# A graph network on one core: one block for all stages, and the first edge group of a relational pass done inside the node pass before it

## The reference, cut to what matters

```python
h = jnp.maximum(_layernorm(x), 0.0)
# twice (w1, sl1, b1, then w2, sl2, b2):
xt  = jnp.einsum('nd,rde->rne', h, W)            # 8 relations
agg = segment_sum(xt[edge_type, src], dst)
h   = relu(agg + h @ SW + b)
x = x + h
h = jnp.maximum(_layernorm(x), 0.0)
e   = relu(concat([h[src], h[dst], edge_attr]) @ eW1 + eb1)
msg = layer_norm(relu(e @ eW2 + eb2), eg, ebeta)
agg = segment_sum(msg, dst)
upd = relu(concat([h, agg]) @ nW1 + nb1) @ nW2 + nb2
out = x + layer_norm(h + upd, ng, nbeta)
```

## Time and profile before

| | us |
|---|---|
| median of the 3 runs | 2733.24 |
| profiled execution, its own time | 2735.01 |
| its span, first to last instruction | 2733.3 |
| TensorE busy | 2139.7 (78%) |
| VectorE busy | 2024.7 (74%) |
| ScalarE busy | 1544.4 (57%) |
| GpSimd (POOL) busy | 1788.3 (65%) |

### The profile page before, as it was taken

One profiled execution on the slowest core, in us unless ns is written; L12 is line 12 of the kernel. 1 busy time (PEld: TensorE's weight loads), 2 busy tenths in 40 slices (PEclk: granted clock), 3 DMA queues, 4 the chain that ended last, 5 costly groups with the idle time before them and its releaser, 6 DMA issues. The chain is left out here.

```text
span 2733.3 us, 54746 instructions
## 1 busy us (share of the span) xinstructions
PE 2139.7 (78%) x16219; PEld 1874.0 (69%) x16219; DVE 2024.7 (74%) x6853; ACT 1544.4 (57%) x3284; POOL 1788.3 (65%) x1381
## 2 busy tenths in 40 slices
PE   3777999999588898888891656577777777648997
PEld 3667999999577798888891655544455544436775
DVE  6887888888333587666662888688777777747999
ACT  4997666666333354444442888645444444426887
POOL 7771777776577188888876777568888888860000
PEclk9999999999899999999995898889888899879999
DMA  6994455555299634444545999877777777739998
GB/s 210 318 323 161 96 103 107 109 109 107 31 340 358 215 73 76 77 85 79 82 56 141 406 417 417 341 230 218 196 189 206 197 200 196 201 72 352 408 409 339
DMA packets 296009, 563.74 MB, mean 206 GB/s; under 512 B 88628, under 2 KB 145377, under 8 KB 295905
## 3 DMA queue, kind: packets, MB, share of 16 engines
q1 hardware_dynamic: 186144, 484.03, 50.9%
q0 software_dynamic: 109760, 78.51, 18.2%
HBM read 368.35 MB, written 205.52 MB: 210 GB/s over the span
## 5 line engine op out<-in xcount | busy, mean ns | idle before, releaser
L1049 POOL DMA_INDIRECT s<-E_summed,c_scat x392 | 637.4, 1626 | 250.9 <-issue 101.5
L1278 PE MATMUL ps<-c_w,E_masked 128*128 128x128 f32 x6272 | 720.4, 276 | 3.9 <-DVE E_masked L1081 3.8
L1278 PEld LDWEIGHTS ps<-c_w,E_masked 128*128 128x128 f32 x6272 | 711.8, 193 | 4.7 <-DVE E_masked L1081 4.7
L1081 DVE SCALAR_TENSOR_TENSOR E_masked<-E_type_row,E_hT 128x512 f32<-128x512 int32 x784 | 483.2, 687 | 78.0 <-ACT E_hT L1198 64.8
L358 POOL DMA_INDIRECT gathered<-s,c_src x392 | 419.0, 1069 | 166.7 <-issue 116.1
L1410 POOL DMA_INDIRECT s<-E_summed,c_scat x196 | 337.4, 1722 | 85.5 <-issue 58.2
L1400 POOL DMA_INDIRECT E_ends<-h,c_near x196 | 202.6, 1034 | 75.8 <-issue 56.1
L358 POOL DMA_INDIRECT gathered<-in_x,c_src x196 | 189.6, 967 | 88.0 <-issue 58.8
L564 PE MATMUL ps<-c_sl,N_hT 128*128 128x128 f32 x1568 | 195.3, 278 | 19.4 <-DVE N_out L399 17.8
L1293 PE MATMUL ps<-E_msg,E_same 128*128 128x128 bf16 (+1 forms) x2450 | 207.3, 241 | 1.2 <-DVE E_msg L1131 1.2
L564 PEld LDWEIGHTS ps<-c_sl,N_hT 128*128 128x128 f32 x1568 | 183.4, 192 | 28.3 <-ACT N_hT L513 21.3
(11 more groups left out here) (133 smaller groups left out, 4461.7 us busy)
## 6 DMA issues: line engine op xcount, KB each, us to landing
s<-N_out SPq DMA_DIRECT2D x147, 512.0 KB, 4.7
N_xin<-in_x SPq DMA_DIRECT2D x98, 512.0 KB, 10.1
N_sin<-s SPq DMA_DIRECT2D x98, 512.0 KB, 6.9
E_dst_row<-in_dst_line SPq DMA_DIRECT2D x147, 256.0 KB, 4.7
E_type_row<-in_type SPq DMA_DIRECT2D x98, 256.0 KB, 4.0
N_xin<-s SPq DMA_DIRECT2D x49, 512.0 KB, 6.4
h<-N_h SPq DMA_DIRECT2D x49, 512.0 KB, 7.8
E_base<-s SPq DMA_DIRECT2D x49, 512.0 KB
```

Source lines behind the costliest of these rows:

```text
L1049: pool.indirect_dma_start(s, bass.IndirectOffsetOnAxis(ap=c["scat"][:, k:k + 1], axis=0), summed[:, g % 2, t * D:(t + 1) * D], None, bound ...
L1081: nc.vector.scalar_tensor_tensor(out=masked[:, u % 2, r, :], in0=type_row[:, u, :], scalar=float(r), in1=hT[:, u % 2, :], op0=ALU.is_equal ...
L1278: ins = nc.tensor.matmul(ps[:, 2 + u % 2, t * D:(t + 1) * D], masked[:, u % 2, r, t * P:(t + 1) * P], w[:, r, :], start=(r == 0 and t == 0 ...
```

## The change

- All stages but the setup stand in one block. `node_product`, `edge_pass_relational` and the others now return a `Stage` of functions, one for each engine, which are called in order in one `nc.Block()`. What the block ends gave is now waited for by name: SP waits for all scatters of an edge pass (`sums_done`) before the first load of the node pass behind it, and POOL waits for the node pass's stores (`all_stored`) before it goes on to the edge pass.
- Group 0 of E1 is worked inside N0, and group 0 of E2 inside N1, by `early_sync`, `early_vector`, `early_scalar` and `early_tensor`, called at the end of each node step: the row loads at step 32, group 0's and 1's statistics, normalisation or copy, and transposes at steps 32 to 41, the masks of groups 0 and 1 two at a time at steps 41 to 48, and group 0's eight products two at a time at steps 43 to 46. In the edge pass TensorE then begins with half of group 1's product and the pairs of group 0.
- The early transposes and products use PSUM banks 6 and 7. The node pass keeps one pair of output banks, 4 and 5, and its product waits half by half for the copy of the group before.
- The node buffers `xin`, `hT` and `out` of N0 and N1 lie in the last 16 slots of `gathered`. So N0 gathers up to group 32 only (N0_AHEAD), and the remaining gathers of an edge pass are spread over its first 42 groups (GATHER_STEPS).
- The node passes' loop ends at group 32 (NODE_LOOP_END = 8); the rest is written out.

The diff without the lines that only move to another indentation:

```diff
-N0_AHEAD = 40
+N0_AHEAD = 32
+NODE_LOOP_END = 8
+GATHER_STEPS = 42
...
-def sweep(eng, step):
+def sweep(eng, step, begin=0, loop_end=LOOP_END):
...
-def node_product(nc, sb, sem, c, ps, a, name, x, s, w, norm, gathers):
+def node_product(nc, sb, sem, c, ps, a, name, x, s, w, norm, gathers, edges, sums_done):
-    xin = sb(f"{name}_xin", [P, UNROLL, NT * D])
-    hT = sb(f"{name}_hT", [P, 2, NT * D])
-    out = sb(f"{name}_out", [P, 2, NT * D])
+    spare = gathers.rows[:, (GROUPS_E - 16) * GE:].rearrange("p (k d) -> p k d", d=NT * D)
+    out, hT, xin = spare[:, 0:2, :], spare[:, 2:4, :], spare[:, 4:8, :]
...
-            copy(out[:, u % 2, h * 512:(h + 1) * 512], ps[:, 4 + 2 * (u % 2) + h, :]).then_inc(out_ready, 1)
+            copy(out[:, u % 2, h * 512:(h + 1) * 512], ps[:, 4 + h, :]).then_inc(out_ready, 1)
...
+                if sums_done:
+                    sp.wait_ge(sums_done, 64 * GROUPS_E)
...
+            edges.early.sync(sp, UNROLL * i + u)
...
     gathers.issue(pool, x, GT * (N0_AHEAD if norm else N1_AHEAD))
+        all_stored(pool, stored)
...
-                wait(pe, out_ready, 2 * (g - 1))
                 for h in range(2):
+                wait(pe, out_ready, 2 * (g - 1) + h + 1)
...
+    def early_sync(sp, at):
+        if isinstance(at, int) and at == 32:
+            for k in range(3):
+                load(sp, 0, k)
...
+        landed = gathers.issued
         for g in range(GROUPS_E):
-                gathers.issue(pool, x, gathers.issued + (1 if norm else 2))
+            gathers.issue(pool, x, TILES_E - (TILES_E - landed) * max(0, GATHER_STEPS - 1 - g) // GATHER_STEPS)
             scatter(g)
...
+    def early_vector(dve, at):
+        if not isinstance(at, int):
+            return
+        if norm and at in (32, 33):
+            k = at - 32
+            rows_here(dve, 0, k)
...
+        if norm and at in (36, 37):
+            shifts(dve, 0, at - 36)
+        if 41 <= at <= 48:
+            masks(dve, 0, (at - 41) // 4, range((at - 41) % 4 * 2, (at - 41) % 4 * 2 + 2))
...
+    def early_scalar(act, at):
+        if not isinstance(at, int):
+            return
+        if norm and at in (33, 34):
+            ln.deviations(nc, act, c["eps"], at - 33, at - 33)
+        if at in (37, 38):
+            if norm:
+                normalise(act, 0, at - 37)
+            else:
+                fetched(act, 0, at - 37)
+        if at in (39, 41):
+            turned_rows(act, 0, (at - 39) // 2)
...
+        if norm:
+            messages(act, 0, 0)
+        equalities(act, 0, 0)
+        if norm:
+            ln.deviations(nc, act, c["eps"], 2, 2)
+            normalise(act, 0, 2)
+        else:
+            fetched(act, 0, 2)
+        sums(act, 0, 0)
+        sweep(act, step, begin=1)
...
+    def early_tensor(pe, at):
+        if not isinstance(at, int):
+            return
+        if at in (38, 40):
+            turn(pe, 0, (at - 38) // 2)
+        if norm and at == 42:
+            pe.wait_ge(c["weights_loaded"], c["weights_all"])
+        if at in (43, 44, 45, 46):
+            multiply(pe, 0, 0, range((at - 43) * 2, (at - 43) * 2 + 2))
...
+        multiply(pe, 0, 1, range(0, 4))
+        add_pairs(pe, 0, 0)
+        turn(pe, 0, 2)
+        multiply(pe, 0, 1, range(4, NREL))
+        sweep(pe, step, begin=2)
+        add_pairs(pe, GROUPS_E // UNROLL, 0)
...
+    with nc.Block() as block:
+        @block.sync
+        def _(sp):
+            n0.sync(sp)
+            e1.sync(sp)
+            n1.sync(sp)
+            e2.sync(sp)
+            n2.sync(sp)
+            e3.sync(sp)
+            n3.sync(sp)
...
```

More of the change, by code:

```diff
@@ new lines, in early_sync, with sync, store_x, step @@
+    def early_sync(sp, at):
+        if isinstance(at, int) and at == 32:
+            for k in range(3):
+                load(sp, 0, k)
+    def sync(sp):
+        def store_x(i, u):
+            g = UNROLL * i + u
+            sp.wait_ge(gathered[u], 64 * (i + 1))
+            sp.dma_start(a["xsrc"][bass.ds(g * P, P), :], gathers.group(g)).then_inc(x_stored, 16)
+        def step(i, u):
+            n = ahead(i, u, 3)
+            if n:
+                load(sp, *n)
+            if norm:
+                store_x(i, u)
+        unrolled(step)
+        if norm:
+            sp.wait_ge(x_stored, 16 * GROUPS_E)
@@ new lines, in rows_here, with shifts, masks @@
+    def rows_here(dve, i, u):
+        g = UNROLL * i + u
+        dve.wait_ge(gathered[u], 64 * (i + 1))
+        wait(dve, normed, g - 3)
+        ln.halves(nc, [gathers.tile(g, t) for t in range(GT)])
+    def shifts(dve, i, u):
+        ln.reciprocals(nc, dve, u, UNROLL * i + u)
+        ln.shifts(nc, u)
+    def masks(dve, i, u, relations):
+        g = UNROLL * i + u
+        if relations[0] == 0:
+            dve.wait_ge(rows_in[u], 32 * (i + 1))
+            dve.wait_ge(hT_ready, g + 1)
+            wait(dve, product, g - 1)
+        for r in relations:
+            nc.vector.scalar_tensor_tensor(out=masked[:, u % 2, r, :], in0=type_row[:, u, :],
+                                           scalar=float(r), in1=hT[:, u % 2, :],
+                                           op0=ALU.is_equal, op1=ALU.mult).then_inc(mask_ready, 1)
@@ new lines, in count_earlier @@
+    def count_earlier(dve, i, u, t):
+        g = UNROLL * i + u
+        if t == 0:
+            dve.wait_ge(rows_in[u], 32 * (i + 1))
+            wait(dve, scat_step, 3 * g)
+        to = (t + 1) * P
+        ins = nc.vector.scalar_tensor_tensor(
+            out=same_block(before, t, 0, t + 1), in0=dst_row[:, u, 0:to], scalar=c["dstf"][:, bass.ds(g * GT + t, 1)],
+            in1=c["earlier"][:, GE - to:GE], op0=ALU.is_equal, op1=ALU.mult, accum_out=count[:, t:t + 1])
+        if t == GT - 1:
+            ins.then_inc(scat_step, 1)
@@ new lines, in normalise, with fetched @@
+    def normalise(act, i, u):
+        g = UNROLL * i + u
+        act.wait_ge(ln.shift_ready, g + 1)
+        wait(act, turned, g - 1)
+        for t in range(GT):
+            ins = ln.scaled(nc, xn[:, u % 2, t * D:(t + 1) * D], gathers.tile(g, t), t, u, ACT.Relu)
+        ins.then_inc(normed, 1)
+    def fetched(act, i, u):
+        g = UNROLL * i + u
+        act.wait_ge(gathered[u], 64 * (i + 1))
+        wait(act, turned, g - 1)
+        nc.scalar.copy(xn[:, u % 2, :], gathers.group(g)).then_inc(normed, 1)
```

1853 lines of the change are left out of this document (917 added, 936 removed).

## The result

The changed kernel takes **2775.66 us** (median of 4 runs, 2771.25 to 2779.33) against 2738.51 before: ratio 1.0141, 95% interval 1.0112 to 1.0169. It is 37 us slower, where 25 us less were forecast. One of the four runs before, at 2799.01 us, was in a slower state, and the ratio leaves it out. The changed kernel's profiled execution took 2778.64 us, its span is 2776.9, or 43.6 above the span before.

The account below looks back on a forecast made before the run. It took no engine to bound all stages: ScalarE and DMA fill N0, TensorE and POOL both limit E1, TensorE N1, POOL E2. Gains of -0.6 (E1 side), 12.9 (E2 side) and 13 (joins) gave 2708 us, range 2686 to 2741.

Parts of the forecast that it names:

- Gathers moved: E1: 32 gathers move in from N0, 25 groups carry a second at 0.62 us; 15.5 us lost (9.8 to 21.8).
- Early work in N0 and N1: Group 0's early work lengthens N0 by 7 us (0 to 13) and N1 by 9 us (5 to 14).
- Group 0 early: E1 and E2: scatter 1 comes sooner after the node pass's last product, gaining 21.9 us in each.
- One block: Joins after three stages ending on a scatter: next loads start 5.6, 4.5 and 3.4 us sooner; gain 13 us.
- Buffers and banks: N0 and N1: node buffers in row slots and a single pair of output banks cost nothing.
- 2689: Rival: second gather hidden in E1 and early work fits in idle time; 44 us gained, 2689 us, chance 0.12.
- The single bank pair: Rival in N0 and N1: copy and product alternate, s us on 98 steps; 2757 us at 0.5, chance 0.10.
- The hand-overs did come earlier: Against the rival that group 0's pairs still wait at N0's end, so only joins gain; 2752 us, chance 0.05.
- POOL is locked out: Rival in E1: each second gather also waits for a mask, 1.23 us instead of 0.62; 2723 us, chance 0.10.
- The sum: Whole kernel: E1 side -0.6, E2 side 12.9, joins 13; 25 us gained together.

Follow-up runs that it names:

- E2: Not a run but a stage of the kernel, the second edge pass; scatter 1 to last scatter 507.2 us before, 508.1 in the changed kernel.
- free_sums: The changed kernel with ScalarE's copy of E1's sums waiting for no scatter (sums go to the row slot of group l-2); 2755.7 us.
- late_rows: The changed kernel with the six early row loads of each node pass two each at steps 33, 39 and 48, not all at 32; 2771.1 us.
- paced40: The changed kernel with 40 groups gathered within N0 again and the early row loads one per step at steps 33 to 38 in both node passes; 2706.0 us.
- few_rows: The changed kernel with N1's six early row loads cut to 32 KB each instead of 256 (some E2 sums wrong); 2766.6 us.
- E3: Not a run but a stage of the kernel, the edge pass after N2; N2 and E3 together 978.9 us before, 983.7 in the changed kernel.
- rows_after_landing: The changed kernel with SP's row loads and stores in E1 held until the scatter of group g-7 has landed; 2737.7 us.

## Why the prediction was wrong, step by step

- **Gathers moved: the step that failed.** It said that POOL sets E1's pace after group 1, and priced a second gather at 0.62 us (0.4 to 0.87), 15.5 us in all; measured 60.7. Both ends of that range took the wait for the landing as a constant that issue either hides or exceeds. But the landing is a transfer, and its time depends on what else is in flight: it was seen 1.72 us after the issue when SP was quiet and 2.73 in the changed kernel, with gaps of up to 6.1 us where the loads went out with the last scatter (free_sums). The wait I reckoned with in E1, 9.88 less 8.94 or 0.9 us a group, comes from a pass whose loads were out of the way. And I noted that two limits lie on each other in E1 without asking what follows: as long as TensorE set the pace, SP's loads went out 0.3 to 1.2 us after a group's first scatter (groups 3 to 34) and were over before its last one landed. A slower GpSimd loses that phase. Even without the collision the moved gathers cost 26.3 us, above the 21.8 that I gave as the most: the gaps, which I did price, 10.9, and the longer issue of the scatters, which I did not, 15.3.
- **Early work in N0 and N1: "SP's six row loads fit in its idle time".** SP's, yes; not the DMA engines', which the earlier trace rows shows 95% busy in N0 and 89% in N1. N0 lost 15.6 instead of 7, N1 16.1 instead of 9. In N0, 7.1 us of the 15.6 lie between stores 31 and 36, where the loads stand; spreading them gave back 4.1 (late_rows) and 5.7 (paced40). The stretch behind store 42, with most of the new matmuls, cost 3.6; the other 4.9 lie before store 31 and between 36 and 42, and no run separates them. In N1 I had counted 1 us for the loads and named 4.7 as what they would cost at the measured rate; few_rows puts them at 6.3. N1's other term, 8 us of new matmuls, is near the 8.7 by which the stretch from store 42 to the end grew.
- **Group 0 early.** The hand-over of E2 shortened by 20.7 us for 21.9 forecast. E1's gave 18.0: scatter 1 stood 27.6 us after N0's last product, not 23.7. I had TensorE go straight on, but its transpose of group 3 waited for ScalarE's normalised rows, and the product of group 2 behind it took 8.94 us instead of 7.31, with the granted clock at 0.50 from 258.5 to 261.8 us:

```profile
257.26 0.66 PE L1329 MATMUL ps<-c_ident,E_xn 128*128 128x128 f32 x4 [2.63 <-ACT E_xn L216]
257.75 8.94 PE L1343 MATMUL ps<-c_w,E_masked 128*128 128x128 f32 x64
```

  In few_rows the wait is the same, the product takes 7.31, and scatter 1 stands at 26.0.
- **One block.** 16.1 us (6.4 + 5.5 + 4.2) for 13. SP's first loads stand 1.5 to 1.7 us after the end of the last scatter's issue, so nearly all of the old 5.9 to 8.1 was the join.
- **Buffers and banks at nothing.** Right: store 31 of N1, ahead of all early work, went out 116.5 us after the pass's first load, 115.9 before; in N0 at 143.3 against 140.4, and at 140.5 in late_rows with the same single bank pair.
- **The rivals.** The time came out slower than three of them gave (2689, 2723, 2752), and none is its main cause. The single bank pair, with 2757 at 0.5 us a step, did not matter. The hand-overs did come earlier, by 18.0 and 20.7 us. "POOL is locked out" I had against the wrong instructions. I argued from a mean of 1.605 us under masks, but that mean mixes two kinds: from group 1 on, 127 of the pass's 192 scatters start inside a VectorE operation with two SBUF inputs and take 1.63 us, up to 2.09, and the other 65 take 1.55. It is mostly scatters that are held up, by up to 0.6 us each, and the issue of E1 grew by 11.6 us in the changed kernel. The Trainium skill (SBUF — State Buffer, Who interferes with whom) has a VectorE instruction with two SBUF inputs contend with a GpSimd instruction that reads SBUF. The trace agrees for a scatter that starts with such an operation under way (2.03 us at 408.87, against 1.56 on average for those that start outside one). It shows nothing of it the other way round: VectorE's masks took 0.69 us beside a scatter and 0.71 without one.
- **The sum.** The forecast was -25, measured +43.6. Of the 69 us between them E1 is 45.2, the two node passes 15.7, the hand-overs 5.1; N2 with E3 and the rest, 6.1, is paid back by half in the joins (3.1). The range reached only to 2741 because I let every cost vary but this one: no rival let the landing wait grow. The time did stay within two per cent, as I gave 0.88 for, but by losses and gains that I had not foreseen.

## What to carry to other kernels

When two engines keep nearly the same pace, the slower one also fixes when everything else runs, as TensorE did in E1; a small cost on the other may hand over the bound, and then transfers meet that did not meet before. Before pricing an added instruction by its own length, look which waits for landings stand behind it, in the stretch itself and not in its tail, and which other transfers are issued around that time. If they collide, a wait on the transfers that are early anyway can be worth a lot: one wait on SP took 34 us off E1 here.

## What the runs showed of the hardware

- A scatter's landing (128 rows of 512 bytes, added in DRAM) was seen 1.72 us after its issue ended with SP quiet (rows_after_landing), 2.73 us with three transfers of 256 KB in flight (the changed kernel).
- A scatter's issue on GpSimd took 1.54 us or, when it started inside a VectorE operation with two SBUF inputs, up to 2.13 us (once 2.68): the more of that operation was left, the longer. The VectorE operation was not longer for it (masks 0.69 us beside a scatter, 0.71 without, in the changed kernel).
- The hole of TensorE in N1 cost more than its length. Around it, in the changed kernel (busy time of PE, granted clock, DMA share, GB/s):

```profile
930.00:939.00 9.00, 0.09 (x1) 0.74 1.00 371
939.40:943.20 3.80, 3.77 (x17) 0.50 0.79 278
```

  After 9.34 us without work the granted clock was 0.50, the lower of the two levels (1.2 GHz), and the next sixteen products took 3.78 us instead of 1.95. From 945 to 960 us it was 1.00 again.
- The trace's name for what ends a wait can be that of a bystander. Two engines waited for one landing, the one that woke first did a copy of 0.6 us, and the other's wait was put down to that copy. Counting which group each instruction belongs to settles it.
